# Splitting the MLP weights slice by slice under the attention loop of a transformer block, on one core

## The reference, cut to what matters

```
mod = swish(c) @ w_mod + b_mod                     # six vectors of 576 per batch
xn  = ln(x) * (1 + sc_msa) + sh_msa
q, k, v = split(xn @ w_qkv + b_qkv);  q = ln(q, g_q);  k = ln(k, g_k)
o   = softmax(q k^T / 6) v                         # 16 heads, 2048 x 2048 each, two batches
x   = x + g_msa * (o @ w_proj + b_proj)
xn2 = ln(x) * (1 + sc_mlp) + sh_mlp
x   = x + g_mlp * (gelu(xn2 @ w1 + b1) @ w2 + b2)
```

## Time and profile before

| | |
|---|---|
| median of 3 runs | 2931.29 us (2931.27 to 2935.87) |
| the profiled execution | 2930.9 us, its span 2929.1 us |
| PE busy | 2793.2 us, 95% |
| DVE busy | 2012.8 us, 69% |
| ACT busy | 1530.7 us, 52% |
| POOL busy | 778.6 us, 27% |
| mean granted clock of TensorE | 0.982 |
| DMA | 157.02 MB, mean 54 GB/s |

### The profile page before, as it was taken

How to read it: one execution, slowest core, us unless ns; L and a number is a source line. 1 busy time by engine, 2 the same in 40 slices (tenths; PEclk the granted TensorE clock), 3 DMA queues, 4 the chain that set the end, 5 groups by cost and what they waited for, 6 DMA issues and landing times.

```text
span 2929.1 us, 43309 instructions
## 1 busy us (share of the span) xinstructions
PE 2793.2 (95%) x14764; PEld 1436.4 (49%) x14764; DVE 2012.8 (69%) x2644; ACT 1530.7 (52%) x2211; POOL 778.6 (27%) x536
## 2 busy tenths in 40 slices
PE   5579999999999999999999998979999999999999
PEld 1334444444444444444444433336575765757666
DVE  5568888888888888888888899964435344343521
ACT  2457777778877777777777787731212112121110
POOL 0143247642223334333333345510000000000000
PEclk9689999999999999999999999989999999999999
DMA  5132222222211111111111132230202202021000
GB/s 171 65 79 54 53 67 76 75 65 51 51 42 34 29 34 29 31 32 29 34 29 34 28 98 68 79 127 22 87 22 66 65 23 87 19 69 60 28 17 17
DMA packets 201782, 157.02 MB, mean 54 GB/s; under 512 B 146982, under 2 KB 147494, under 8 KB 201522
## 3 DMA queue, kind: packets, MB, share of 16 engines
q1 hardware_dynamic: 201356, 155.12, 19.3%
q10 hardware_dynamic: 296, 0.07, 0.0%
HBM read 87.49 MB, written 34.09 MB: 42 GB/s over the span
## 4 chain that ended last, share of the span: by engine, by line
PE 88%; DVE 6%; ACT 1%; issue 1%; POOL 1%; DMA 0%; SPq 0%; DVEq 0%; ACTq 0%; POOLq 0%
PE at_ps L1462 18%; PE at_ps L1487 15%; PE at_ps L847 14%; PE at_ps L844 14%; PE at_ps L835 14%; PE at_ps L863 10%; DVE at_plo L703 4%; PE at_ps L901 1%; PE at_ps L1452 1%; ACT at_p L607 0%; ACT at_aff L631 0%; PE at_ps L874 0%; DMA ml_den<-head_den 0%; DVE ml_w2s L1415 0%; POOL at_ssq L527 0%
## 5 line engine op out<-in xcount | busy, mean ns | idle before, releaser
L703 DVE TENSOR_TENSOR at_plo<-at_p 128x1024 fp32r<-128x1024 f32 x1024 | 1281.9, 1277 | 205.6 <-ACT at_p L607 203.8
L607 ACT ACTIVATE at_p<-at_ps 128x1024 f32<-128x1024 f32 x1024 | 1046.8, 1026 | 434.4 <-PE at_ps L835 434.0
L847 PE MATMUL at_ps<-at_plo,at_vr 128*37 128x512 f32 x2048 | 1073.4, 592 | 0.0
L844 PE MATMUL at_ps<-at_p,at_v 128*73 128x512 bf16 x2048 | 797.5, 389 | 20.7 <-DVE at_plo L703 20.6
L1462 PE MATMUL at_ps<-ml_w2s,ml_hid 128*128 128x288 f16 x3456 | 428.1, 286 | 2.0 <-issue 2.0
L1487 PE MATMUL at_ps<-ml_xhi,ml_w 128*128 128x512 f16 x1296 | 399.3, 381 | 3.4 <-issue 3.4
L1462 PEld LDWEIGHTS at_ps<-ml_w2s,ml_hid 128*128 128x128 f16 x3456 | 338.0, 98 | 86.9 <-issue 2.5
L513 POOL TENSOR_TENSOR at_tssq<-at_tssq,head_eps 128x8 f32<-128x8 f32 x112 | 124.2, 1109 | 926.2 <-DVE at_tssq L677 926.2
L844 PEld LDWEIGHTS at_ps<-at_p,at_v 128*73 128x73 f16 x2048 | 232.7, 114 | 271.1 <-DVE at_plo L703 20.7
L847 PEld LDWEIGHTS at_ps<-at_plo,at_vr 128*37 128x37 f32 x2048 | 233.6, 114 | 219.8 <-issue 0.5
L863 PE MATMUL at_ps<-wq,at_xhi 128*128 128x432 f16 x1008 | 297.6, 350 | 19.0 <-DVE at_txc L681 18.5
(11 more groups left out here) (159 smaller groups left out, 2396.3 us busy)
## 6 DMA issues: line engine op xcount, KB each, us to landing
head_sums<-at_oT SPq DMA_DIRECT2D x256, 72.0 KB
ml_held<-head_sums SPq DMA_DIRECT2D x64, 256.0 KB
at_xy<-in_x SPq DMA_DIRECT2D x32, 288.0 KB, 2.8
ml_x<-in_x SPq DMA_DIRECT2D x8, 1152.0 KB, 5.6
out<-ml_x SPq DMA_DIRECT2D x7, 1152.0 KB, 4.5
wm<-in_L_cond_w_mod SPq DMA_DIRECT2D x6, 1152.0 KB, 13.9
ml_held<-head_rden SPq DMA_DIRECT2D x24, 216.0 KB
normal_rows<-at_xy SPq DMA_DIRECT2D x16, 320.0 KB, 2.2
```

The lines of the kernel that those rows point to most:

```text
L607: act.activation(p[:, s % NP, :], ps[:, 2 * (s % 2):2 * (s % 2) + 2, :].rearrange("p a n -> p (a n)"), ACT.Exp).then_inc(exp_done, 1)
L703: nc.vector.tensor_tensor(plo[:, s % NP, :], p[:, s % NP, :], high, ALU.subtract).then_inc(plo_ready, 1)
L844: nc.tensor.matmul(acc[0:VW, bass.ds((U % 2) * CH, CH)], v16[:, h % 2, 2 * s + a, 0:VW], high, start=(s == 0 and a == 0), stop=False, skip ...
L847: last = nc.tensor.matmul(acc[0:RW, bass.ds((U % 2) * CH, CH)], vr[:, h % 2, 2 * s + a, 0:RW], plo[:, s % NP, a * CH:(a + 1) * CH], start= ...
```

## The change

1. The float32 weights w_proj with its bias, w1 and w2 are cut into 44 slices of at most 128 rows by 576 columns (6, 20 and 18). In each of the 44 units that begin with group 4 (all of groups 4 and 5, 12 units of group 6) SP loads one slice into `xy`, ACT makes its high half in step 5 (`word_high`, 128x576), DVE its low half in step 5 (`word_lower`, 128x576), and SP stores both halves in DRAM. The halves are laid in columns of `wq` that are no longer read.
2. Group 7 no longer splits anything: ACT's 33 `high_part`, POOL's 40 operations of `low_rows` and DVE's `low_tail` are gone. SP loads the halves of w_proj in unit 0 (`load_wp`, 1.3 MB) and those of w1 in unit 5 (`load_w1`, 5.3 MB). The gates are loaded in unit 7 (before: 14).
3. In the MLP stage `load_w2` loads 5.3 MB of halves, and the lots are gone.
4. In the first chunk DVE takes statistics and normalises tile by tile (`first_project`, `first_normal`), and POOL makes rstd one column at a time. `low_x` follows the reciprocal directly.

```
+            def word_high(i):
+                act.wait_ge(w_loaded, 16 * i + 16)
+                act.wait_ge(w_stored, 32 * i + 32)
+                act.activation(word_hi, word, ACT.Copy, scale=WS).then_inc(w_high, 1)
...
+            def word_lower(i):
+                dve.wait_ge(w_high, i + 1)
+                nc.vector.scalar_tensor_tensor(out=word_lo, in0=word, scalar=WS, in1=word_hi, op0=ALU.mult, op1=ALU.subtract).then_inc(w_low, 1)
...
+                i = U - SLICED * UNITS
+                if 0 <= i < SLICES:
+                    src = slices[i][0]
+                    if i == 0:
+                        sp.wait_ge(n_lo, NT + 1)
+                    else:
+                        sp.wait_ge(w_low, i)
+                    sp.dma_start(xy[0:src.shape[0], 0:H], src).then_inc(w_loaded, 16)
...
+                if 0 <= i < SLICES:
+                    src, half, r0, cols = slices[i]
+                    n = src.shape[0]
+                    sp.wait_ge(w_low, i + 1)
+                    for h, part in enumerate((word_hi, word_lo)):
+                        sp.dma_start(half[h, r0:r0 + n, cols].rearrange("p (a n) -> p a n", a=2), part[0:n]).then_inc(w_stored, 16)
                 if G == GROUPS - 1:
+                    if u == 0:
+                        sp.wait_ge(w_stored, 32 * SLICES + 32)
                     rest.sync_early(sp, u)
...
-                if G == GROUPS - 1:
-                    rest.gpsimd_early(pool, u)
...
-            self.load_piece(sp, 0)
-            self.load_piece(sp, 1)
             self.load_den(sp, 0)
+            self.load_wp(sp)
...
-        if u in (5, 8, 11):
-            self.load_piece(sp, u // 3 + 1)
-        if u == 14:
-            self.wait_low(sp, self.PIECES - 1)
+        if u == 5:
+            self.load_w1(sp)
+        if u == 7:
             sp.dma_start(self.gates[:, :, :, :].rearrange("p b v n -> p (b v n)"), bcast(self.gates_dram, 0, P)).then_inc(self.gates_loaded, 16)
...
-        if 1 <= u < 4 and s in (1, 4, 6):
-            self.high_part(act, 0, 3 * (u - 1) + (1, 4, 6).index(s))
-        if u >= 4 and s in (2, 6):
-            self.high_part(act, (u - 4) // 3 + 1, 2 * ((u - 4) % 3) + (2, 6).index(s))
...
-        if u in (4, 7, 10, 13) and s == 7:
-            self.low_tail(dve, u // 3 - 1)
...
+    def load_w1(self, sp):
+        w1, rows = self.w1, lambda half, r0, r1: self.halves.w1[half, r0:r1, :]
+        for half in range(2):
+            sp.dma_start(w1[:, half * KF:(half + 1) * KF, :], rows(half, 0, KF * P).rearrange("(k p) n -> p k n", p=P)).then_inc(self.w1_loaded, 16)
+            sp.dma_start(w1[half * KT:(half + 1) * KT, 8, :], rows(half, KF * P, H)).then_inc(self.w1_loaded, 16)
...
+        def first_project():
+
+            dve.wait_ge(self.x_loaded, 16)
+            for i in range(TPC):
+                residual(0, i, i, 0, self.x1_ready)
+                dve.wait_ge(self.x1_ready, i + 1)
+                for h in range(2):
+                    last = nc.vector.bn_stats(self.stats[:, i, h, :], self.x1[:, i, h * HALF:(h + 1) * HALF])
+                last.then_inc(self.first_stats, 1)
+                if i:
+                    first_normal(i - 1)
+                dve.wait_ge(self.first_stats, i + 1)
+                nc.vector.bn_aggr(self.mv[:, i, :], self.stats[:, i, :, :].rearrange("p a b -> p (a b)")).then_inc(self.first_mv, 1)
+            first_normal(TPC - 1)
...
-        self.low_tail(dve, self.PIECES - 1)
+        nc.vector.memset(self.xlo[KT:P, KF, :], 0.0).then_inc(self.xlo_zero, 1)
         dve.wait_ge(self.gates_loaded, 16)
-        project(0, 0)
+        first_project()
         self.invert_den(dve, 1)
-        lot_low(0)
-        lot_low(1)
-        self.wait_low(dve, self.PIECES)
-        nc.vector.memset(self.xlo[KT:P, KF, :], 0.0).then_inc(self.xlo_zero, 1)
         low_x(0, range(KC))
```

More of the change, by code:

```diff
@@ L421, in attention_mlp @@
             sem("n_" + n) for n in ("loaded", "stats", "mv", "var", "rstd", "y", "whole", "stored"))
+        w_loaded, w_high, w_low, w_stored = sem("w_loaded"), sem("w_high"), sem("w_low"), sem("w_stored")
+        SLICED = NG
+        SLICES = Mlp.SLICES
+        word = xy[:, 0:H].rearrange("p (a n) -> p a n", a=2)
+        word_hi, word_lo = wq[:, 0:2, 0:HALF], wq[:, 2:4, 0:HALF]
+        slices = ([(w_proj[k * P:min((k + 1) * P, H), :], halves.wp, k * P, slice(0, H)) for k in range(KC)] + [(b_proj.unsqueeze(0), halves.wp, H, slice(0, H))] +
+                  [(w1[k * P:min((k + 1) * P, H), c0:c0 + H], halves.w1, k * P, slice(c0, c0 + H)) for c0 in range(0, MLP, H) for k in range(KC)] +
+                  [(w2[f * P:(f + 1) * P, :], halves.w2, f * P, slice(0, H)) for f in range(FT)])
         ny_loaded, n_turned, n_aff, n_hi, n_lo = (sem("n_" + n) for n in ("y_loaded", "turned", "aff", "hi", "lo"))
@@ L426, in attention_mlp @@
         ends = Ends(t_mm, t_stored, scores_ready, head_ready, pv_done, exp_done, oT_ready, oT_stored, n_lo)
-        rest = Mlp(nc, ctx, keep, place, ps, ends, x, sums_dram, den_dram, rden_dram, out, w_proj, b_proj, w1, b1, w2, gates_dram)
+        rest = Mlp(nc, ctx, keep, place, ps, ends, x, sums_dram, den_dram, rden_dram, out, halves, b1, gates_dram)
         block = ctx.enter_context(nc.Block())
@@ L621, in unit @@
                         hats_high(u)
+                    if sliced and s == 5:
+                        word_high(U - SLICED * UNITS)
                     if G == GROUPS - 1:
@@ L722, in unit @@
                         nc.vector.tensor_tensor(xlo[0:KT, KF, tok], xy[0:KT, KF * P:], xhi[0:KT, KF, tok], ALU.subtract).then_inc(n_lo, 1)
+                    if sliced and s == 5:
+                        word_lower(U - SLICED * UNITS)
                     if G == GROUPS - 1:
@@ L1008, with __init__ @@
     WITH_DOWN = ((0, 1), (2, 3), (4,), ())
-    def __init__(self, nc, ctx, keep, place, ps, ends, x, sums_dram, den_dram, rden_dram, out, w_proj, b_proj, w1_in, b1, w2, gates_dram):
+    def __init__(self, nc, ctx, keep, place, ps, ends, x, sums_dram, den_dram, rden_dram, out, halves, b1, gates_dram):
         sb = lambda n, s, d, at: place("ml_" + n, s, d, at)
@@ L1082, in tr_bank @@
         return self.ps[:, 6 + k % 2, :]
[L1084 to L1096, removed]
     def credits(self):
@@ L1389, in project, with first_normal @@
             last.then_inc(self.y_ready, 1)
+        def first_normal(i):
+            dve.wait_ge(self.first_rstd, i + 1)
+            row = self.x1[:, i, :]
+            for c0, c1, at in ((0, H, 0), (KF * P, H, H)):
+                last = nc.vector.tensor_scalar(self.tok[:, i, at:at + c1 - c0], row[:, c0:c1], self.mv[:, i, 0:1],
+                                               self.rstd[:, 1, i:i + 1], ALU.subtract, ALU.mult)
+            if i == TPC - 1:
+                last.then_inc(self.y_ready, 1)
+        def first_project():
+            dve.wait_ge(self.x_loaded, 16)
+            for i in range(TPC):
+                residual(0, i, i, 0, self.x1_ready)
[8 more added lines that the diff above has]
+            first_normal(TPC - 1)
         def low_x(J, ks):
```

174 lines of the change are left out of this document (58 added, 116 removed).

## The result

The changed kernel took 2892.84 us (median of 4 runs, 2892.19 to 2893.01) beside 2931.28 for the kernel before: ratio 0.9868, 95% interval 0.9856 to 0.9880, faster by 38.4 us (35 to 42). The forecast was 2897.5, 33.8 us faster, with 2887 to 2920 as its range. Its profiled execution took 2893.01 us against 2930.9, with spans of 2891.1 and 2929.1.

A forecast was written before the change was run, and what follows sets the result against it. PE was 88% of the chain of waits, DVE 6%, so only DVE stretches could be gained; -26.1 (group 7) + 2.6 (groups 4 to 6) - 10.3 (MLP start) = -33.8 us, giving 2897.5 us, range 2887 to 2920.

The forecast's parts named there:

- rival (d): More gain: `up` at full clock from its start (3 us), group 7 and slices costing nothing (1.5 each): 2891.5 us; 7%.
- the first `up`: First `up` of the MLP stage: left at 57.40 us and clock 0.95, change between 0 and -3 us.
- Group 7: Group 7 without splitting work: from 201.74 to 175.6 us, -26.1 us, with 1.5 us of stalls allowed.
- The floor of 174.1 us: Group 7's 128 PE steps at 1.36 us each, the spacing of two steps where DVE kept up.
- The loads: Weight loads in group 7: `load_w1` takes 16.2 us, needed 21.8 us after it began, cover 5.6 us; cost 0.
- one of its signs: Sign for the loads: L580 (`keep_oT` on ACT) waits for no DMA in units 6 and 7.
- Groups 4 to 6: 44 units get one ACT and one DVE operation each: 0.06 us a unit, +2.6 us in all.
- Rival (a): In groups 4 to 6 POOL's power holds the new DVE operation, 0.98 us a unit, 43 us: 2941 us; 5%.
- Rival (b): In groups 4 to 6 POOL's power is let in only after the new DVE operation: 22 us, 2919 us; 8%.
- Start of the MLP stage: Between project and `up`: tile-by-tile normalisation and no lots let `up` start at 1939.6 instead of 1949.91, -10.3 us.
- The bound of 9 us for group 7: Upper bound on group 7's stalls: fifteen attention output operations and three `head` copies, each held by 0.5 us.

The follow-up runs named there:

- Experiments 1 to 3: Kernel before with, in turn: POOL's group 7 splitting cut to one column (2908.64 us); DVE's low tails left out (2926.47 us); POOL's splitting done by DVE (2911.20 us).
- Experiment 3: Kernel before, with POOL's 40 splitting operations of group 7 done by DVE instead, in 20 operations: 2911.20 us, ratio 0.9929.
- experiment 9: Changed kernel with 40 extra matmuls into an unused bank in the gap between the first project and the first `up`: 2892.81 us.
- experiment 5: Changed kernel with every slice's DVE operation done twice in step 5, the second copy into unused columns: 2919.91 us.
- experiment 7: Changed kernel with the low halves of the 44 slices made by POOL, in two operations each, instead of DVE: 2899.51 us.
- experiment 8: Changed kernel with POOL's additions of the gates in the first chunk put behind the last `low_x`: 2893.74 us.
- experiment 1: Kernel before, with POOL's 40 splitting operations of group 7 cut to one column each, PE reading high halves for low ones: 2908.64 us.

## Why the prediction was right, step by step

The kernel gained 38.1 us in the profiles where 33.8 were forecast. Of the 4.3 us between them 2.6 are the slices, 1.1 the start of the MLP stage, 0.75 a chance difference ahead of group 0 and 0.2 the first `up`; group 7 is 0.3 the other way. The time, 2892.84, is nearer to rival (d), 2891.5, than to the forecast, 2897.5. But the largest term of (d), a first `up` at the full clock, did not come: `up` took 57.25 us at 0.95, as before.

**Group 7** (-26.1 forecast, -25.8 measured). The floor of 174.1 us, taken from two steps in which PE waited for nothing, was 2.3 us below the measured 176.42, where 1.5 of stalls had been allowed. Only 0.5 of the 2.3 are PE's idle time (176.42 - 175.90); the rest is its own work, and no run divides it. Experiments 1 to 3 divide the gain: 22.6 us without POOL's work alone, some 4.0 without the tails, and at most 3.2 for the tails, ACT and one-column operations together. The prediction took away POOL and the tails together and said that DVE would then just keep up. Experiment 3 shows how near the edge that was: with the 20 operations, some 15 us of work, and the tails on DVE, 6.3 us were back.

**The loads** (0, and 0.2 to 0.4). This term was nearer its edge than the forecast had it, and one of its signs failed. The four loads of w1's halves took 20.9 us together, from the issue of the first (1766.14) to the landing of the last (1787.07), not the 16.2 forecast and just under the 21.8 of cover. The store behind them was still late: ACT waited for it once (L602 is `keep_oT`, the old L580), at 1787.6, in unit 7 (us in total, times, longest):

```profile
ACT at_oT L602 <- DMA head_den<-at_oT: 1.2, 1, 1.2
```

Of the 1.2 us, 0.17 reached PE as idle time. In experiment 9 the load took 20.8 us, ACT waited 1.1, and group 7 took 176.30 us. In the six other profiles with these loads they took 16.9 to 19.1 us, ACT did not wait for a store, and group 7 took 176.02 to 176.06 us, 0.4 less than 176.42. So the load's length differs between executions, and the longest ones cost a few tenths; why is not shown.

**Groups 4 to 6** (+2.6, and 0.0). This is the term that was mis-sized. I carried 0.06 us a unit from group 0 as the price of such an operation. In this loop the price is what goes beyond the idle time on the path. These are the rows of DVE and POOL of the changed kernel in group 5, for the steps of the earlier trace rows, and PE's next product.

```profile
1340.36 2.35 DVE L742 TENSOR_TENSOR at_plo<-at_p 128x1024 fp32r<-128x1024 f32 x2
1342.64 0.75 DVE L730 SCALAR_TENSOR_TENSOR wq<-at_xy,wq 128x576 f16<-128x576 f32 x1
1343.32 1.21 DVE L742 TENSOR_TENSOR at_plo<-at_p 128x1024 fp32r<-128x1024 f32 x1
1344.45 0.44 DVE L716 SCALAR_TENSOR_TENSOR at_txc<-at_ps,at_tssq 128x288 f32<-128x288 f32 x1
...
1341.71 2.50 POOL L539 TENSOR_TENSOR at_tssq<-at_tssq,power 128x8 f32<-128x8 f32 x1
...
1345.08 0.54 PE L911 MATMUL at_ps<-wq,at_xhi 128*128 128x432 f16 x2
```

POOL's power still ends at 1344.21, 0.24 before L716 starts, so L716's wait of 0.33 us for it is used up. From the end of L716 to PE's product 0.19 us are left (1344.89 to 1345.08). That is close to what a release takes: in experiment 5, where PE waits for L716, it starts 0.15 us behind its end in most units and 0.06 in the others. The new operation needs 0.68 us, and the path held 0.08 more (0.68 - 0.60 by experiment 5), so 0.76. Group 0's operations push DVE by 0.84 in the unit of the earlier trace rows (0.72 for the two statistics, 0.12 for an aggregate in step 5). By this sum, an estimate, that is 0.08 too much, against the 0.06 measured there, and 0 here. No run tested group 0 itself.

**Rival (a), DVE held by POOL's power.** It did not come: L730 takes 0.75 us with the power running, and in experiment 5 two of them, 0.75 each and over by 1341.89, fit into one power (1339.54 to 1342.04). The Trainium skill (SBUF — State Buffer, section "SBUF: two separate sides") says that a DVE operation with two SBUF inputs and a POOL operation that reads SBUF exclude each other for the whole instruction. The traces agree for POOL's 128x576 subtraction, beside which L748 took 2.30 us instead of 1.22 in experiment 7. They do not agree for its power on 128x8, nor for its 128x576 scaling, beside which L748 took 1.22 us, though both read SBUF; here the measurement decides. **Rival (b)** did not come either: the power lasts 2.50 us as before.

**Start of the MLP stage** (-10.3, and -11.4). The gap is 0.6 us shorter than forecast, as POOL's one-column pair keeps DVE idle for 0.93 us instead of the 1.5 that I took from four columns. From the transposes to `up` it was 9.3 instead of 9.8 us: I had added 1.1 us for POOL's blocking, and experiment 8 measures it at 0.6.

**Two slips in the working.** The bound of 9 us for group 7 uses 0.5 us a held operation and calls it half of 1.17 - 0.7; that is the whole of it. Rival (d) takes 1.5 us off for the slices, whose term was 2.6, so its time should be 2890.4. Neither changes the forecast.

**What was luck**: 0.75 us came ahead of group 0, where nothing was changed; the profiles of all kernels have that point between 184.9 and 187.7 us, so it is no effect of the change.

## What to carry to other kernels

In this loop, work beside it was free up to the idle time that its engine had between the place where it was put and the operation that the bounding engine waits for, and cost its length beyond that (0.00, 0.21 and 0.60 us a unit for one and the same operation). Count that stretch, not the engine's busy share. Before work is moved off an engine that looks full, see whether its operations are long by their own amount or by waiting for another engine: here DVE could take over POOL's work and still become 17 us less busy. A price measured near such a limit says whether the limit is passed, and cannot be scaled by the length. When two executions of the same code differ by a few us, read the granted clock of the stretch before looking for a wait.

## What the runs showed that I had not expected

- The work after the first `up` takes 921.95 us in six of the profiles and 923.63 in seven others, in kernels with the same code there, and the last chunk's `down` 53.09 us or 54.77. The granted clock explains the size. In all seven it is at 1.2 GHz for 3.41 us soon after that `down` begins, and in none of the six; half of 3.41 is 1.7. Here are these 3.41 us in experiment 9 and the same place in the kernel before, with 16 matmul records and 30:

```profile
2834.34:2837.75 3.41, 3.41 (x16) 2.07 (x15) 0.00 (x0) 0.00 (x0) 0.00 (x0) 0.50 0.00 0
...
2873.25:2876.66 3.41, 3.41 (x30) 2.72 (x29) 0.00 (x0) 0.00 (x0) 0.00 (x0) 1.00 0.00 0
```

PE stands idle for 2.01 us just ahead of that `down` in both. Why the clock falls behind it in some executions and not in others is not shown. It hides effects of under 2 us in a single profile.
- POOL's power -1/2 took 0.55 us on 128x1, 1.02 on 128x4 and 1.64 on 128x8: about 0.15 us for each column beside a fixed 0.4.
- One column on POOL is not cheap either: in experiment 1 the one-column scaling took 1428 ns in the mean, though the shortest of the 20 took 222 ns. So most of that mean is waiting; for what, the rows do not say.
